# A two-layer network with gated delta rule: the triangular inverse on half-width tiles, and its last level issued in turns

## What is computed

```python
mixed = hidden_states @ W_qkv
z = (hidden_states @ W_z).reshape(B, T, NV, DV)
beta = sigmoid(hidden_states @ W_b)
g = -exp(A_log) * softplus(hidden_states @ W_a + dt_bias)
conv = sum((xp[:, i:i + T, :] * conv_w[:, i] for i in range(KC)))   # 4 taps
q, k, v = split(silu(conv))                                          # l2-normed q, k
def step(S, xs):                                                     # scan over T
    S = S * exp(gt)
    kS = einsum('bhk,bhkv->bhv', kt, S)
    S = S + bt * kt * (vt - kS)
    o = einsum('bhk,bhkv->bhv', qt, S)
o = o * rsqrt(mean(o * o) + 1e-6) * norm_w * silu(z)
return o.reshape(B, T, value_dim) @ W_out
```

## Time and profile before

| | us |
|---|---|
| median of 3 runs | 2122.12 |
| lowest, highest | 2114.63, 2125.47 |
| the profiled execution | 2117.74 |
| its span, first to last instruction | 2115.8 |
| TensorE busy | 1917.6 (91%) |
| VectorE busy | 1505.7 (71%) |
| ScalarE busy | 984.2 (47%) |
| GpSimd busy | 759.0 (36%) |

### The profile page before, as it was taken

How to read it: one execution, slowest core, us unless ns; L and a number is a source line. 1 busy time by engine, 2 the same in 40 slices (tenths; PEclk the granted TensorE clock), 3 DMA queues, 4 the chain that set the end, 5 groups by cost and what they waited for, 6 DMA issues and landing times.

```text
span 2115.8 us, 43478 instructions
## 1 busy us (share of the span) xinstructions
PE 1917.6 (91%) x15082; PEld 1402.3 (66%) x15082; DVE 1505.7 (71%) x2430; ACT 984.2 (47%) x2535; POOL 759.0 (36%) x685
## 2 busy tenths in 40 slices
PE   4578886888799999999999999999999999999998
PEld 3246662333555687877878778787687777877877
DVE  5786771111677687787787877878778787787887
ACT  1012224777213354645545455455564555645544
POOL 4730002110300334616336164362543624526343
PEclk9689998999899999999999999999999999999999
DMA  6635661000122200010010000100001001010010
GB/s 245 209 91 200 184 178 55 26 20 1 55 60 70 82 17 35 5 35 30 15 35 10 30 30 15 35 30 10 30 15 35 30 10 40 5 35 30 15 45 20
DMA packets 75254, 111.75 MB, mean 53 GB/s; under 512 B 23318, under 2 KB 56742, under 8 KB 72006
## 3 DMA queue, kind: packets, MB, share of 16 engines
q1 hardware_dynamic: 71694, 102.32, 15.1%
q0 software_dynamic: 3072, 8.39, 1.3%
q10 hardware_dynamic: 446, 0.48, 0.1%
HBM read 85.80 MB, written 28.52 MB: 54 GB/s over the span
## 4 chain that ended last, share of the span: by engine, by line
PE 51%; DVE 16%; issue 4%; ACT 3%; POOL 0%; DVEq 0%; ACTq 0%; POOLq 0%
PE ps L1273 5%; PE ps L1311 4%; PE ps L1321 4%; DVE conv L1862 3%; DVE P L2034 3%; DVE P_term L2031 3%; PE ps L1544 3%; PE ps L1493 3%; PE ps L1533 3%; PE ps L1428 3%; PE ps L1417 3%; PE ps L1546 3%; PE ps L1520 2%; PE ps L1450 2%; PE ps L1525 2%
## 5 line engine op out<-in xcount | busy, mean ns | idle before, releaser
L1862 DVE SCALAR_TENSOR_TENSOR conv<-raw,tap_st,conv 128x1024 f32<-128x1024 f32 x204 | 299.5, 1468 | 3.6
L1273 PE MATMUL ps<-xnT,w_conv_st 128*128 128x512 f32 x544 | 247.6, 599 | 0.0
L1842 POOL TENSOR_TENSOR o<-o,silu_z 128x256 f32<-128x256 f32 x128 | 138.5, 1082 | 255.5 <-DVE silu_z L1882 141.7
L816 DVE TENSOR_REDUCE m_part<-ps 128x1 f32<-128x640 f32 (+7 forms) x176 | 176.4, 1027 | 67.1 <-PE ps L667 53.5
L1726 POOL TENSOR_TENSOR gmask_Q<-upto,g 128x2048 f32<-128x2048 f32 x17 | 61.4, 3611 | 363.5 <-PE ps L1500 335.5
L998 ACT ACTIVATE probs<-ps 128x1024 f32<-128x1024 f32 (+7 forms) x256 | 145.9, 660 | 58.1 <-PE ps L933 28.7
L1273 PEld LDWEIGHTS ps<-xnT,w_conv_st 128*128 128x128 f32 x544 | 98.9, 191 | 101.1 <-issue 96.2
L1565 ACT COPY raw<-ps 128x512 f32<-128x512 f32 x136 | 80.7, 594 | 173.4 <-PE ps L1273 173.4
L1822 POOL TENSOR_TENSOR kq_decayed<-conv,decay_rows 128x1024 f32<-128x1024 f32 x64 | 159.3, 2521 | 0.0
L1321 PE MATMUL ps<-w_z_st,xnT 128*128 128x256 f32 x512 | 148.8, 393 | 0.0
L903 POOL DMA_INDIRECT slot_outputs<-scratch_slots_y,token_slots x32 | 30.6, 958 | 310.9 <-POOLq L496 202.0
(11 more groups left out here) (345 smaller groups left out, 4728.9 us busy)
## 6 DMA issues: line engine op xcount, KB each, us to landing
decay_rows<-scratch_egc SPq DMA_DIRECT2D x17, 1024.0 KB, 4.7
w_conv_st<-in_w_conv SPq DMA_DIRECT2D x17, 512.0 KB, 3.3
scratch_slots_x<-yacc SPq DMA_DIRECT2D x8, 1024.0 KB, 14.9
slot_rows<-scratch_slots_x SPq DMA_DIRECT2D x16, 512.0 KB, 4.7
scratch_slots_y<-slot_outputs SPq DMA_DIRECT2D x16, 512.0 KB, 3.4
w_gate_up<-in_gu SPq DMA_DIRECT2D x8, 768.0 KB
w_gate_up<-in_gu SPq DMA_DIRECT2D x32, 192.0 KB
kq_decayed<-in_gu SPq DMA_DIRECT2D x22, 256.0 KB, 2.8
```

What stands on the lines that cost most here:

```text
L816: dve.tensor_reduce(dst, src, AX.X, ALU.max).then_inc(s_max, 1)
L1273: mm = pe.matmul(ps[:, 6 + n % 2, :], wc[:, k, (n // 2) * P:(n // 2 + 1) * P], m.xnT[:, k, (n % 2) * HALF:(n % 2 + 1) * HALF], start=k == ...
L1842: g.tensor_tensor(oc, oc, zs[:, c, :], ALU.mult).then_inc(s_oz, 1)
L1862: op = dve.scalar_tensor_tensor(out=cv[:, t, :], in0=raw[:, t, at:at + T], scalar=tap[:, t, at:at + 1], in1=cv[:, t, :], op0=ALU.mult, op1 ...
```

## The change

Seven edits to the loop:

1. Q and P of the levels are kept as 64-wide diagonal halves only: `qd` and `pd`, [128, 2, 8, 64] each, both in the room of `gm_q`. Masks and the block spreads shrink to half (`bmask4`, `lmask`); X becomes 32 wide (`xs32`).
2. A transpose turns two chunks at once (`pd[:, e, 2j:2j+2]` is 128 wide); the blocks land in other halves, and ScalarE picks them up in four pieces (`halves`). `place` says for each level, chunk and half which partitions, bank and slot a product uses; `base` gives each head its banks. In the second level X goes by its input half to different banks, and by the parity of the chunk to the upper or lower 64 partitions; Y takes its input from the half of the chunk's parity and writes the two output halves.
3. Last level: head 0's X, the z projection, then head 1's X and head 0's product with P in alternation, chunk by chunk, then `project(i+1, 7)` (before inside the first level), then head 1's product.
4. Seam on TensorE: kk banks 0, 1; two output turns; kk banks 2, 3; two output projections; two turns; the rest; the last two projections after `turn_v(0)`; four projections of the next head before P instead of five.
5. Seam on VectorE: taps 1 to 3 of tile 3 of head i at the very start of turn i (before in the scan of the turn before), then L2010, then `gate_outputs`, then the silu of tile 3, `add_out(0)`, the U steps, `add_out(1..3)`. The masking reads the blocks from PSUM (`U_BANK`), to which ScalarE now copies them; the addition of the halves is a reduction of one operand. The identity for `pc` is laid by ScalarE.
6. GpSimd copies the taps after `kq_decayed` instead of at the turn's end; ScalarE's `tanh_conv` of tiles 1 and 3 move.
7. The masks of the first layer are made for 2 levels instead of 7, on GpSimd.

```diff
+        xs32 = xs[:, :, 0:NC // 2, :].rearrange("p e c (q n) -> p e (c q) n", q=2)
+        gm_room = gm_q[:].rearrange("p e c n -> p (e c n)")
+        qd = gm_room[:, 0:NC * P].rearrange("p (e c n) -> p e c n", e=2, c=NC)
+        pd = gm_room[:, NC * P:].rearrange("p (e c n) -> p e c n", e=2, c=NC)
...
+        def place(lv, c, h):
+
+            j, hi = c // 2, int(h is HI)
+            if lv == FIRST:
+                return h, c, 0, c, 0, c
+            return (LO, HI)[c % 2], 2 * j + hi, hi, j, c % 2, j
+
+        def halves(e):
+
+            turned = ps[:, 2 + e, :].rearrange("p (j h n) -> p j h n", h=2, n=64)
+            return [(h, odd, turned[(LO, HI)[odd], :, int(h is HI), :]) for h in (HI, LO) for odd in range(2)]
+
+        def base(lv, e):
+
+            return (e, (4, 0)[e], (4, 1)[e])[lv - FIRST]
...
                 for b in range(4):
+                    if b == 2:
+                        pe.wait_ge(s_e, i * 4 + 4)
+                        for n in range(2):
+                            turn_outputs(i, n)
                     for c in (2 * b, 2 * b + 1):
...
-                pe.wait_ge(s_e, i * 4 + 4)
-                for n in range(4):
+                for n in range(2):
+                    project_out(i, n)
+                for n in range(2, 4):
                     turn_outputs(i, n)
-                for n in range(3):
-                    project_out(i, n)
...
-                for n in range(5):
+                for n in range(4):
                     project(i + 1, n)
...
-                    for c in range(NC):
-                        mm = pe.transpose(ps[:, 2 * e + c // 4, (c % 4) * P:(c % 4 + 1) * P], e_p[:, e, c, :], m.ident[:])
+                    for j in range(NC // 2):
+                        mm = pe.transpose(ps[:, 2 + e, j * P:(j + 1) * P], pd[:, e, 2 * j:2 * j + 2, :].rearrange("p c n -> p (c n)"), m.ident[:])
...
-                                dst = ps[h, e, c * 64:(c + 1) * 64].rearrange("p (b s) -> p b s", s=s)
-                                mm = pe.matmul(dst, ua[h, e, c, 1, h], gm_q[h, e, c, :].rearrange("p (b t s) -> p b t s", t=2, s=s)[:, :, 0, :],
+                                g, at, bank, slot, _, _ = place(lv, c, h)
+                                dst = ps[g, bank + base(lv, e), slot * 32:(slot + 1) * 32].rearrange("p (b s) -> p b s", s=s)
+                                mm = pe.matmul(dst, ua[h, e, c, 1, h], qd[h, e, c, :].rearrange("p (b t s) -> p b t s", t=2, s=s)[:, :, 0, :],
...
-                                mm = pe.matmul(ps[h, e, c * 64:(c + 1) * 64], e_p[h, e, c, h], xs[h, e, c, :], start=True, stop=True)
+                                g, at, _, _, bank, slot = place(lv, c, h)
+                                mm = pe.matmul(ps[h, bank + base(lv, e), slot * 32:(slot + 1) * 32], pd[g, e, at, :], xs32[g, e, at, :], start=True, stop=True)
...
+                pe.wait_ge(s_yt, i * NT + NT - 1)
+                pe.sem_inc(s_passed, 1)
+                for c in range(NC):
+                    mm = corner(0, c)
+                mm.then_inc(s_x, 1)
+                project_z(i, 0)
...
+                for c in range(NC):
+                    mm = corner(1, c)
+                    py = corner_p(0, c)
+                mm.then_inc(s_x, 1)
+                py.then_inc(s_y, 1)
+                project(i + 1, 7)
...
+                for c in range(NC):
+                    mm = corner_p(1, c)
+                mm.then_inc(s_y, 1)
                 for j in range(2):
                     turn_kq(i + 1, j)
...
+                pool.wait_ge(s_conv, i * 4 + 4)
+                passed()
+                g.tensor_copy(tap[:], m.taps[:, bass.ds(i + 1, 1), :, :].rearrange("p a b c -> p (a b) c")).then_inc(s_taps, 1)
...
-                gate_outputs(i, 1)
+                for k in range(1, TAPS):
+                    conv_op(i, 3, k)
                 dve.wait_ge(s_e, i * 4 + 4)
...
-                for n in range(3):
-                    add_out(i, n)
+                gate_outputs(i, 1)
+                conv_op(i, 3, TAPS)
+                add_out(i, 0)
...
-                dve.tensor_tensor(uc[:], u32[:, :, 0, :], u32[:, :, 1, :], ALU.add).then_inc(s_uc, 1)
-                add_out(i, 3)
+                dve.tensor_reduce(uc[:], u32[:].rearrange("p u t i -> p u i t"), AX.X, ALU.add).then_inc(s_uc, 1)
+                for n in range(1, 4):
+                    add_out(i, n)
...
-                        + [(1, TAPS)] + [(2, k) for k in range(TAPS)] + [(3, 0), (3, 1), (2, TAPS), (3, 2), (3, 3), (3, TAPS)])
+                        + [(1, TAPS), (2, 0), (2, 1), (2, 2), (2, 3), (3, 0), (2, TAPS)])
...
-                        if e == 0:
-                            more(1)
...
-                    more(3)
+                    more(3 if lv == FIRST else 2)
...
-                silu_z(i, 0)
-                more(1)
+                    if e == 0:
+                        silu_z(i, 0)
+                more(2)
```

More of the change, by code:

```diff
@@ L1490, in _ @@
                     for e in range(2):
                         pe.wait_ge(s_yt, i * NT + n0 + e + 1)
[L1492 to L1493 removed]
+                        for j in range(NC // 2):
+                            mm = pe.transpose(ps[:, 2 + e, j * P:(j + 1) * P], qd[:, e, 2 * j:2 * j + 2, :].rearrange("p c n -> p (c n)"), m.ident[:])
                         mm.then_inc(s_t, 1)
[L1496 to L1501 removed]
@@ L1502, in _, with corner @@
-                pe.wait_ge(s_pt, i * ND + NT)
-                project_z(i, 0)
-                for e in range(2):
-                    pe.wait_ge(s_xt, i * ND + NT + e + 1)
-                    pe.wait_ge(s_pt, i * ND + NT + e - 1)
-                    pe.sem_inc(s_passed, 1)
-                    for c in range(NC):
-                        mm = pe.matmul(ps[LO, e, c * 64:(c + 1) * 64], xs[HI, e, c, :], e_p[HI, e, c, HI], start=True, stop=True)
-                    mm.then_inc(s_y, 1)
+                def corner(e, c):
+                    return pe.matmul(ps[HI, base(LEVELS - 1, e), c * 64:(c + 1) * 64], ua[LO, e, c, 1, HI], qd[LO, e, c, :], start=True, stop=True)
@@ new lines, in corner_p @@
+                def corner_p(e, c):
+                    return pe.matmul(ps[LO, base(LEVELS - 1, e), c * 64:(c + 1) * 64], xs[HI, e, c, :], e_p[HI, e, c, HI], start=True, stop=True)
+                pe.wait_ge(s_yt, i * NT + NT - 1)
[4 more added lines that the diff above has]
+                project_z(i, 0)
+                pe.wait_ge(s_yt, i * NT + NT)
+                pe.wait_ge(s_xt, i * ND + NT + 1)
@@ L1659, in _ @@
                     nc.scalar.activation(chunks(e_p[:, b // 2, 4 * (b % 2):4 * (b % 2) + 4, :]), ps[:, b, :], ACT.Exp).then_inc(s_e, 1)
-                for n in range(4):
+                tanh_conv(i, 3)
+                for n in range(2):
                     turn_out(i, n)
+                nc.scalar.copy(pc[:], eye1[:].unsqueeze(1).broadcast_to([P, UNITS, BLK])).then_inc(s_ch, 1)
                 act.wait_ge(s_u, i * 4 + 4)
@@ L1665, in _ @@
                     rows = slice(32 * q, 32 * q + 32)
-                    nc.scalar.copy(u32[rows].rearrange("p u t i -> p u (t i)"), uu[rows, :, rows]).then_inc(s_u32, 1)
+                    nc.scalar.copy(ps[rows, U_BANK, :].rearrange("p (u n) -> p u n", u=UNITS), uu[rows, :, rows]).then_inc(s_u32, 1)
+                for n in range(2, 4):
+                    turn_out(i, n)
                 act.wait_ge(s_rk, i * 5 + 1)
-                act.wait_ge(s_ch, i * SUBS)
                 nc.scalar.copy(a1b[:].rearrange("p u i -> p (u i)"), ps[:, A1_BANK, 0:UNITS * BLK]).then_inc(s_u32, 1)
@@ L1679, in _ @@
                     act.wait_ge(s_qt, i * 2 + e + 1)
-                    nc.scalar.copy(chunks(gm_q[:, e]), two_banks(2 * e)).then_inc(s_q, 1)
-                    copy_raw(i + 1, 5 + e)
+                    for h, odd, src in halves(e):
+                        last = nc.scalar.copy(qd[h, e, odd::2, :], src)
+                    last.then_inc(s_q, 1)
+                    copy_raw(i + 1, 4 + e)
                 tanh_conv(i + 1, 0)
@@ L1795, in _ @@
             totals(0)
-            pool.wait_ge(s_conv, 4)
-            passed()
-            g.tensor_copy(tap[:], m.taps[:, 1]).then_inc(s_taps, 1)
-            pool.wait_ge(s_dve, 5)
+            pool.wait_ge(s_dve, 7)
             passed()
```

105 lines of the change are left out of this document (60 added, 45 removed).

## The result

The changed kernel takes **2157.41 us** (median of four runs, 2155.99 to 2157.92), the kernel before 2122.55 beside it (2114.63 to 2125.47): a ratio of **1.0172, interval 1.0151 to 1.0194**. Slower by 1.7%, where 2131 was forecast and the range ended at 2156. The profiled execution took 2157.92 us, span 2156.0 (before 2115.8), and the granted clock is 0.949 over the span (before 0.976).

What follows compares the result with a forecast made beforehand. A turn is TensorE's work plus some 3 us of waits; +0.75 - 0.15 = +0.6 us a turn, x 16 = +9.6, -0.5 at the loop's end, gives 2126.8 profiled; the median, 4.4 above, 2131 us; range 2094 to 2156.

Steps and rivals of the forecast that it cites:

- TensorE's clear part: TensorE's work in a turn: half the transposes go (-2.7 us), last-level corners alternate (-1.0 us); sum -3.7 us a turn.
- the place of L1450: Seam on TensorE: L1450 reached at 18.1 us into the turn without its 0.95 us wait, -1.0 us.
- the reduction: Seam on VectorE: the sum of halves as a one-operand reduction takes 0.65 us for 2.45.
- two steps of the chain under the lock: VectorE's chain before P: two of 15 steps pass till 24.5 us beside GpSimd's L1822; P ready at 33.7.
- both waits: TensorE stalls 3.7 us before P's transposes, released by VectorE's spread, and 2.1 us before turn_kq, released by the tap operation.
- the mechanism of the locks: GpSimd operations and VectorE ones with two SBUF operands exclude each other for a whole instruction; L1726 holds tile 1's tap operation.
- rival 1: The locks bite less: turn_kq starts at 57.1 us, -2.1 us a turn, 2097 us; chance 0.18.
- the start of the scan: After turn_kq, the scan starts 60.15 us into the turn, before at 59.4.
- The term of the X and Y products: The two levels' products with 32 moving columns for 64: no gain taken, bounds 0 and -4.1 us a turn.
- Rival 3: Second-level products sharing a row half lose their overlap: +1.0 us a turn, 2147 us; chance 0.13.
- the tap operations that the change moves out of it save nothing there: Stage before the loop: it is solid TensorE (40.00 of 40.00 us), so moving tap operations out saves nothing.
- The forecast's case: Whole kernel: +0.6 us a turn, 2131 us, within 2118 to 2144 by when P comes; chance 0.42.

Runs made afterwards that it cites:

- Filled waits: The changed kernel with useless 512-column TensorE products, four before P's transposes and two before turn_kq: 2111.55 us, ratio 0.9964.
- products in halves: The changed kernel with GpSimd's gate product cut in four and each of its four products with the decays in two: ratio 0.9776.
- only the products with the decays cut: The changed kernel with each of GpSimd's four kq products (L1874) cut in four, gate product whole: ratio 0.9815.
- the kernel with the later gate product: The changed kernel with GpSimd's gate multiplication for the next head waiting until that head's tile 1 is complete: 2122.52 us, ratio 1.0019.
- The kernel with both splits: The changed kernel with GpSimd's gate product and each of its four products with the decays cut in four: 1996.29 us, ratio 0.9585.
- the kernel before with split products: The kernel before with GpSimd's gate product and each of its four products with the decays (L1822) cut in four: 2056.61 us, ratio 0.9859.
- eighths: The changed kernel with GpSimd's gate product cut in four and each of its four products with the decays in eight: ratio 0.97.

## Why the prediction was wrong

**The sum.** *Right:* TensorE's clear part (half the transposes; the alternating corner in 1.08 us, forecast 1.02); the place of L1450 (17.8 us into the turn, forecast 18.1); the reduction (0.70 us, 0.65); two steps of the chain under the lock, and P at 33.4 us (33.7); both waits, by size, place and releaser. By the mechanism of the locks the turn was forecast within 0.4 us at each of these points, and rival 1, that they bite less, was wrong. *Right by luck:* the start of the scan, at 59.8 us (60.15). Between P and the scan two misses of 1.4 us cancel: the half clock behind the first wait and the faster products, both below.

**The term that failed is one that the sum didn't have: TensorE's clock behind a wait.** I put a wait of 3.7 us and one of 2.1 into an engine that had been at a clock of 1.00, and costed both at their length only. Each halves the clock for the work behind it. Filled waits take off 3.03 us a turn. Where the clock falls only in some turns, those are longer by 1.41 us behind the first wait (products in halves, last section) and by 84.69 - 83.02 = 1.67 behind the second (only the products with the decays cut), 3.08 in sum; in the kernel with the later gate product the loss behind the first is nothing, 1.5 or 2.35 us by the turn. No row of before could show it in the steady turns, since the longest wait there was 0.95 us. Just behind the last turn one does:

```profile
2100.09 5.38 PE L1311 MATMUL ps<-w_out_st,xn_nat 128*128 128x256 f32 x16 [1.62 <-ACT xn_nat L1598]
```

The same 16 instructions take 3.72 us when they come again at 2107.26, and the granted clock from 2100.09 to 2102.50 is 0.50. So the trace of before had a price for a wait, and I didn't look for it. The Trainium skill (TensorE: Matmul & The Clock Gate, Why this matters for your kernels) warns that idle gaps between bursts in mid-kernel bring the clock down; behind both waits here, 3.63 and 2.00 us, it was down.

**The term of the X and Y products** was the miss of the other sign. I took no gain from them, between 0 and -4.1 us. The reasoning (columns don't set the pace) was right in the main and stands measured; what I overlooked is that the new layout of the second level visits four quadrants where there were two. It takes 1.14 us for 2.05 in two groups of a turn, and TensorE had to wait 0.52 us for VectorE's copy inside and 0.54 for ScalarE's before the alternating group: from P to the scan some 1.4 us less, net. The kernel with both splits shows it without a stall or a lower clock: from P to turn_kq it takes 1377.87 - 1355.76 = 22.1 us, where the steps of the prediction add up to 57.1 - 33.7 = 23.4. Rival 3 said the opposite of the same pairs, that they would lose their overlap, since both products of a chunk take their rows from one half; they run at 16 ns an instruction (64 weight loads in 1.05 us), though a single record lasts 0.2 us. The Trainium skill's rule (TensorE: Matmul & The Clock Gate, Part 3), that a weight load overlaps only where the row group differs, doesn't hold for them. Of the floor of about 25 ns between starts that the prediction quotes these groups say only this: 16 ns between records, 32 ns between products, which have two records each.

So per turn: 87.43 forecast, -0.3 for P's time, -1.4 for the products, +1.4 and +1.6 for the clock behind the two waits: 88.75.

**The first turn (6.8 us)** failed at one sentence: "the tap operations that the change moves out of it save nothing there". I asked what leaving costs, not what arriving costs. I worked out where the three operations go in a steady turn, where GpSimd starts L1816 only at 8.9 us; in the first turn it starts at once.

**Before the loop (4.7 us).** Left open. On the chips of the second kind the changed kernels begin the loop between 671.4 and 679.9 us and the kernel before with split products at 674.9, so nothing shows that the change costs time there.

**The chances.** The forecast's case was the right one but for the clock; the range was built from how much the locks bite, and no case held a cost that multiplies a wait.

## What to carry to other kernels

A wait that you put into a saturated TensorE costs its length and, with the 2 to 3.6 us of these, often also the half clock behind it (mostly 1.4 to 1.7 us, up to 2.35): price both, or fill the wait. Where GpSimd and VectorE share a stretch, look at the length of one GpSimd instruction before you look at order: cutting them to about the length of VectorE's step gave 5.8% against the changed kernel (0.9585 for 1.0172), where it took two waits and the clock's loss away, and 1.4% in the kernel before, which had neither; moving them gave 1.5% or nothing. When operations move into a loop, cost the first turn by itself.

## What the hardware showed that I hadn't expected

- The same wait doesn't always cost the clock. With products in halves two turns in a row wait 2.86 and 2.82 us before P; behind the first L1296 takes 1.88 us, behind the second 2.81, and the turns take 82.89 and 84.30 us. In the changed kernel all but one of the 15 turns with the long wait before P lost it there. Behind 2.00 us before turn_kq it was lost in 10 of 16 turns where only the products with the decays are cut, behind 2.2 us before P in only 2 of 15 with eighths. So the length of the wait alone doesn't decide it, and no run here shows what does.

```profile
1382.13 0.66 PE L1490 MATMUL ps<-ident,gmask_Q 128*128 128x128 f32 x4 [2.86 <-DVE gmask_Q L2106]
1382.62 1.88 PE L1296 MATMUL ps<-xnT,w_conv_st 128*128 128x512 f32 x4
...
1465.01 0.66 PE L1490 MATMUL ps<-ident,gmask_Q 128*128 128x128 f32 x4 [2.82 <-DVE gmask_Q L2106]
1465.50 2.81 PE L1296 MATMUL ps<-xnT,w_conv_st 128*128 128x512 f32 x4
```

- The pace of 64x64 products is 63 ns, about 31 ns or about 16 ns an instruction by one, two or four quadrants in turn, with 32 columns much as with 64.
- Cutting a GpSimd product of 128x1024 costs about 0.2 us for each further piece beside VectorE's chain (12.88 for 10.44 us with 12 pieces more, 15.16 with 28 more). The gate product of 128x2048 in four takes 6.45 us for 3.61, with VectorE's tap operations beside it, 0.9 us for each further piece.
